# A two-layer graph network on one core: the load of x in 112 + 15 partitions, the copy of src in 128 rows and a rest

## The reference, cut to what matters

```python
h = relu(layernorm(x))
x = x + relu(h @ W_self + segment_mean(h[src], dst) @ W_neigh + b)        # layer 0
h = relu(layernorm(x))
hid = relu(concat(h[src], h[dst]) @ We1 + be1)                            # layer 1, per edge
m = sigmoid(hid @ We2 + be2) * h[src]
msgs = concat(segment_max(m, dst), segment_sum(m, dst))
x = x + relu(concat(msgs, h) @ Wn1 + bn1) @ Wn2 + bn2 + h
```

## Time and profile before

| | us |
|---|---|
| median of 3 runs | 8183.52 |
| lowest and highest of them | 8175.11 and 8204.45 |
| the profiled execution's own time | 8185.29 |
| its span | 8183.6 |

### The profile page before, as it was taken

One profiled execution on the slowest core, in us unless ns is written; L12 is line 12 of the kernel. 1 busy time (PEld: TensorE's weight loads), 2 busy tenths in 40 slices (PEclk: granted clock), 3 DMA queues, 4 the chain that ended last, 5 costly groups with the idle time before them and its releaser, 6 DMA issues.

```text
span 8183.6 us, 111687 instructions
## 1 busy us (share of the span) xinstructions
PE 3724.8 (46%) x24938; PEld 3291.0 (40%) x24939; DVE 4329.6 (53%) x8524; ACT 2902.3 (35%) x4472; POOL 3814.0 (47%) x3768
## 2 busy tenths in 40 slices
PE   0006999999963333333433433333333333343341
PEld 0005888888853333333333333333333333333331
DVE  2746888888854444444544444445444444444441
ACT  4005888888852222222222222222222222222220
POOL 2461000000026666565555555556555555555555
PEclk9999999999975555555555555555555555555555
DMA  3320000000012222222222222222222222222221
GB/s 109 100 48 21 19 18 19 19 19 19 19 40 68 68 65 67 66 67 67 63 66 66 63 64 66 66 63 66 63 64 65 61 62 65 62 65 64 62 65 27
DMA packets 298529, 455.47 MB, mean 56 GB/s; under 512 B 124801, under 2 KB 220264, under 8 KB 298336
## 3 DMA queue, kind: packets, MB, share of 16 engines
q0 software_dynamic: 178784, 375.77, 17.2%
q1 hardware_dynamic: 88308, 50.07, 2.2%
q10 hardware_dynamic: 31402, 29.21, 1.1%
HBM read 385.93 MB, written 40.42 MB: 52 GB/s over the span
## 4 chain that ended last, share of the span: by engine, by line
another core or an unknown queue 25%; PE 24%; issue 17%; DVE 16%; DVEq 9%; ACT 5%; DMA 1%; POOL 1%; ACTq 1%; SPq 0%; POOLq 0%; PEld 0%
PE ps_acc L1378 8%; PE ps_acc L1408 8%; PE ps_pairs L1400 6%; DVE act_w L1108 5%; DVEq L402 4%; DVE chunk_max L1125 3%; ACT counts_f L1267 3%; DVE msg L1119 2%; DVEq L1119 1%; DVE pre L1102 1%; DVEq L1167 1%; DVE z L1114 1%; DVEq L1102 1%; POOL out_dram L533 1%
## 5 line engine op out<-in xcount | busy, mean ns | idle before, releaser
L458 POOL DMA_INDIRECT counts_f<-hA_table,stage x3264 | 3287.2, 1007 | 2346.4 <-issue 971.1
L1378 PE MATMUL ps_acc<-msg,ident 128*128 128x64 f32 (+1 forms) x6508 | 1633.7, 429 | 2536.9 <-DVE msg L1119 2109.9
L1378 PEld LDWEIGHTS ps_acc<-msg,ident 128*128 128x128 f32 x6508 | 1462.1, 326 | 2708.4 <-DVE msg L1119 2025.4
L1267 ACT ACTIVATE counts_f<-ps_pairs 128x784 bf16<-128x784 f32 x1568 | 1270.1, 823 | 311.4 <-PE ps_pairs L1400 244.8
L1119 DVE TENSOR_TENSOR msg<-counts_f,gate 128x256 f32<-128x256 f32 x851 | 359.5, 422 | 1719.8 <-remote 1494.2
L1343 ACT ACT_TABLE_LOAD x834 | 1070.0, 1283 | 259.0 <-DMA own<-own_rows 174.5
L1343 ACT ACTIVATE gate<-z,be_col 128x4 f32<-128x4 f32 x851 | 253.1, 297 | 2232.6 <-DVE z L1114 1584.5
L1408 PE MATMUL ps_acc<-pieces_f,counts_f 128*128 128x192 bf16 x9604 | 1014.6, 246 | 0.7 <-ACT counts_f L1267 0.4
L1400 PE MATMUL ps_pairs<-hot 128*128 128x196 bf16 x6272 | 818.3, 252 | 142.4 <-ACT counts_f L1267 136.2
L521 POOL DMA_INDIRECT hA_table<-node,node_id x98 | 131.8, 1345 | 1610.0 <-ACT node L1278 1575.6
L1408 PEld LDWEIGHTS ps_acc<-pieces_f,counts_f 128*128 128x128 bf16 x9604 | 879.4, 138 | 1.4 <-issue 1.3
(11 more groups left out here) (206 smaller groups left out, 2997.3 us busy)
## 6 DMA issues: line engine op xcount, KB each, us to landing
counts_f<-hA_table,stage POOLq DMA_INDIRECT x3264
counts_f<-counts_f SPq DMA_DIRECT2D x102, 288.0 KB
own_rows<-node ACTq DMA_DIRECT2D x98, 128.0 KB
own<-own_rows ACTq DMA_DIRECT2D x98, 128.0 KB
xh<-records SPq DMA_DIRECT2D x98, 64.0 KB, 1.8
stage<-stream SPq DMA_DIRECT2D x206, 8.0 KB
h_table<-counts_f ACTq DMA_DIRECT2D x14, 224.0 KB
stream<-runs_m SPq DMA_DIRECT2D x14, 224.0 KB
```

The costliest lines, as they stand in the source:

```text
L458: return pool.indirect_dma_start(to, None, table, bass.IndirectOffsetOnAxis(ap=idx, axis=axis))
L1267: act.activation(counts[:, c, nodes, :].rearrange("p (b h) t -> p b (h t)", h=2), ps_pairs[g & 1][:, :].rearrange("p (b w) -> p b w", b=BA ...
L1378: return pe.matmul(ps_sum[:, 0:D], ident[:, :], rows, start=False, stop=False, skip_group_check=True)
```

## The change

The one load of x by 127 partitions becomes two, of 112 and of 15 partitions; the one copy of src becomes one of 128 rows of 3222 numbers and one of the last 84. The two constants that are waited for grow by 16 each. Nothing else differs.

```diff
-        TAB_DMAS = 16 * 2
-        X_DMAS = 16 * (2 if REST else 1)
+        TAB_DMAS = 16 * 3
+        X_DMAS = 16 * (3 if REST else 2)
...
-            sp.dma_start(x_nodes[0:FULL], x[0:FULL * T, :].rearrange("(p t) d -> p t d", p=FULL)).then_inc(s_x, 16)
+
+            by = FULL // 16 * 16
+            sp.dma_start(x_nodes[0:by], x[0:by * T, :].rearrange("(p t) d -> p t d", p=by)).then_inc(s_x, 16)
+            sp.dma_start(x_nodes[by:FULL], x[by * T:FULL * T, :].rearrange("(p t) d -> p t d", p=FULL - by)).then_inc(s_x, 16)
             if REST:
                 sp.dma_start(x_nodes[FULL:FULL + 1, 0:REST], x[FULL * T:N, :].unsqueeze(0)).then_inc(s_x, 16)
             flat_src = src_pad.rearrange("a b -> (a b)")
-            sp.dma_start(flat_src[0:E], src[:]).then_inc(s_tab, 16)
+            even = E // P * P
+            sp.dma_start(flat_src[0:even].rearrange("(a b) -> a b", a=P),
+                         src[0:even].rearrange("(a b) -> a b", a=P)).then_inc(s_tab, 16)
+            sp.dma_start(flat_src[even:E].unsqueeze(0), src[even:E].unsqueeze(0)).then_inc(s_tab, 16)
```

## The result

The changed kernel takes 8082.34 us (median of 4 runs, 8065.82 to 8086.67) against 8193.99 for the kernel before (4 runs, 8175.11 to 8205.71): a ratio of 0.9862, 95% interval 0.9836 to 0.9889. It is faster by 1.4%, between 1.1 and 1.6%. The forecast was 8079. The profiled executions stand at 8086.67 and 8185.29, 98.6 us apart; the medians are 111.7 us apart.

What follows compares the result with a forecast made beforehand. One DMA engine carrying all of x was taken to pace the search for 150 us; the last gather at 163 instead of 268.81 us saves 106, so 8185.3 - 106 = 8079 us, range 8055 to 8120.

Steps and rivals of the forecast that it cites:

- The turn of 1.51 us: Search gathers, kernel before: one piece of x and one gather packet alternate on the loaded engine, 12.1 / 8 = 1.51 us.
- first rival: Load of x: the fifteen rows go to one engine, busy until about 44 us; 8087 us, chance 0.05.
- the upper bound: Load of x, kernel before: 127 pieces at 1.18 us beside gathers, from about 13 us, end at 163 us.
- Fifteen rows on fifteen engines: Second load of x: its 15 partitions give one more piece to each of fifteen engines.
- x by 22.4 us, SP's queue empty by 26: Start: eight pieces of x per engine take 9.4 us from 13; src then takes 3.8 us.
- the worse case of the prediction: Start: x at 255 GB/s takes 12.5 us, so x is in at 25.5 us and SP's queue empty at 29.
- The free pace of 1.40 us: Rest of the search: 89 gathers at 1.40 us each, 124.9 us, from the eleventh at 36.8 us.
- Behind the search: From last gather to end: the remainder of 7914.8 us moves forward whole, keeping the 106 us gain.
- Swallowed: Behind the search: a wait read as slack is not, above all ACT's weights; up to 8185 us, chance 0.05.
- no gain: Load of x: splitting by partitions gains nothing, both parts using the same sixteen engines; 8185 us, chance 0.02.
- slower: Layer 1: two more SP instructions delay its 102 gather groups; 8283 us at 2 us a group, chance 0.02.
- The pace of 2.0 us beside ACT's passes: Search: gathers take 2.0 us with ACT at work, last at 215 us, gain 54, 8131 us; chance 0.04.

Runs made afterwards that it cites:

- the dose of 66 pieces: Changed kernel with x loaded in 64, 61 and 2 partitions instead of 112 and 15: 7980.74 us, against 8021.41 for the kernel before.
- halves: Kernel before, with x as two loads of 49 columns, each of 127 partitions: 6719.33 us against 6731.68.
- quarters: Kernel before, with x as four loads of 24 or 25 columns, each of 127 partitions: 6703.45 us against 6731.68.
- the late load: Changed kernel with x, still split in 112 and 15, loaded only after the search's last gather landed: 7911.93 us against 8021.41 for the kernel before, ratio 0.9871.
- the late whole load: Changed kernel with x loaded after the search as one load of 127 partitions: 7998.38 us against 7914.56 for the changed kernel.

## Why the prediction was right

*The cause.* One engine with 127 pieces of x, taking turns with every gather. Shown from both sides: moving the cut by one partition brings the pairs 12 us apart back, splitting src alone leaves them, the dose of 66 pieces has them without a long hold of SP, and the length of the pieces sets their distance.

*The turn of 1.51 us.* The mechanism was right and this figure of it was not: it came from dividing the 12.1 us of a pair by eight packets. The DMA view of the kernel before from 47.1 to 52.8 us, when the other fifteen engines have nothing left to do, shows the loaded engine by itself:

```profile
DMA packets 10, 0.15 MB, mean 26 GB/s; under 512 B 1, under 2 KB 1, under 8 KB 5
q1 hardware_dynamic: 5, 0.13, 5.1%
q0 software_dynamic: 5, 0.02, 0.9%
```

Five pieces and five packets of gathers, in strict turn: a piece takes 0.94 us and a packet of 5,000 bytes 0.19, a turn of 1.13. One of the five packets is not data but 4 bytes long, and takes next to nothing. With it a gather has five packets on the engine and a pair ten, so ten pieces of x pass with each pair. The packet records from 42.8 to 54.8 us have these ten turns: five of 1.13 us (or 1.12), two of 0.94, and three longer ones of 1.63, 1.63 and 1.24 us while the next pair moves on the other engines, 12.0 us in all. The forecast did not hang on the 1.51, save for the backlog of its first rival; the expectations for halves and quarters did. For the same reason x ended a little beyond the 163 us of the upper bound, at 167.4, or 1.21 us a piece.

*Fifteen rows on fifteen engines.* Right: the packet records have fifteen of these pieces in flight together, in the changed kernel (at 23.9 us) as in the late load. The Trainium skill ("DMA: Bandwidth & Descriptors", section on why a DMA increments its semaphore by 16) states the rule, the largest number up to 16 that divides the slowest dimension, here the rows. All cuts tried agree: 127, 113 and 61 behave like one engine, 112 and 64 like sixteen, 63 like nine, 15 like fifteen. The advice of the Trainium skill (same page, rules for kernel authors) against cutting a transfer by partitions did not hold here, with a ratio of 0.9848 for x alone; it presumes that the whole transfer already uses sixteen engines.

*x by 22.4 us, SP's queue empty by 26.* Here a term was mis-sized. Even the 266 GB/s of the best five us are near the low bound of 255 and far from the single engine's rate times sixteen; x took 15.1 us instead of 9.4 (11.9 to 27.0; alone in the late run 14.8), and the large pieces of src lasted to 32.0. Both ends lie beyond the worse case of the prediction, 25.5 and 29. It cost nothing, and that is in part luck: ACT's second pass covers up to 34 us, which left 2 us to spare; the eleventh gather left at 37.84 for 36.8, and 37.33 without x.

*The free pace of 1.40 us.* It was (167.12 - 37.84) / 89 = 1.45, so the last gather was 4.1 us later than 163: 1.0 us from the later eleventh gather, and 3.1 from the pace (129.3 us for 89 gathers, against 124.9 and the 1.3 added for the weights).

*Behind the search.* 7917.8 us for 7914.8: the remainder moved forward whole, as said, but for 3 us. With the 4.1 of the search that makes the 7 us between 8079 and the profiled 8086.67. The median, 8082.34, lies nearer, by the spread of the runs. ACT's slack was 78.5 us.

*The rivals.* Swallowed, no gain and slower are excluded by the ratio. The pace of 2.0 us beside ACT's passes did not come; why it stays above POOL's own 1.25 is open (last section). Fifteen rows on one engine is excluded by the packet records.

## What to carry to other kernels

Look at the DMA share of a queue, multiplied by sixteen: a steady 0.85 (beside gathers) or 1.02 (alone, the 6.4% of the late whole load) is one engine, and all three loads with a prime number of partitions tried here, 127, 113 and 61, looked like that. The cost in this kernel was not the load's own length, which was hidden, but that every evenly spread gather beside it finished with the slowest engine. The gain can be estimated as the time of that engine's load, less what the others needed anyway: gathers 11 to 33 took 130 us, and 22 gathers at 1.45 take 32, which leaves 98, and the eleventh itself came 4 us earlier. Before splitting further, see whether the first cut already fits under something else: here 8, 11 or no pieces on an engine ahead of the first gathers put the eleventh at 37.8, 42.0 and 37.3 us.

## What the runs showed of the hardware that was not expected

*Stalls with no releaser.* In the changed kernel VectorE and ACT stand still several times in the search, and the profile names nothing that they wait for. At times they do so together (VectorE stands from 84.5 to 87.1 us, ACT for 1.2 us of it), at times not: ACT went on for most of VectorE's longest such wait. That wait, and ACT's last search count:

```profile
108.66 0.17 DVE L707 TENSOR_SCALAR row<-balance  x1 [4.68 <-issue]
```
```profile
120.86 0.18 ACT L1223 ACTIVATION_READ_ACCUMULATOR hot<-pieces_f,q_mid  x1
```

ACT does the same hundred counts as before and needs 6 us more for them, although it waits for no gather. Nine passes in the kernel before, beside DMA engines that the gathers and x kept busy for 29% (23.6 and 5.3), were 10.1 us each without exception. VectorE has such stalls in the free stretch of the kernel before too, 20 us in all from 177 to 270, so the 1.40 us contain them. In the kernel with halves the free stretch ran without them, 42 gathers in 52.97 us, 1.26 us each, which is POOL's own issue cadence, at a DMA share of 0.85. So full DMA engines alone don't bring them about; but that run was on another chip. What the stalls are was not tried.

*Sixteen engines are not sixteen times one.* A piece of 25,088 bytes took 0.92 us on an engine alone before the gathers, and 0.94 in the late whole load, where one engine carried the 127 pieces in 119 us. With x late and split, sixteen engines carried the same 127 pieces in 14.8 us: eight times as fast, not sixteen. A piece then took 1.70 us on the mean; in the best five us it was 1.5 (16 x 25,088 bytes at 266 GB/s), and the last fifteen took 2.2 to 3.3 us. What sets this limit was not tried.

*Three levels of the same kernel.* The kernel before took 8194, 8021 to 8037, and 6732 us in different groups, and the three groups of experiments ran on three chips. The difference to the last level lies in layer 1. The stretch of the earlier trace rows from 2400 us has 3255 gathers in 5750 us; the kernel with halves, of the last group, has this (columns as in the earlier trace rows) for the whole stage:

```profile
2350.00:6600.00 4250.00, 2158.40 (x8075) 1826.90 (x8074) 2553.12 (x5604) 1401.29 (x1979) 3248.36 (x3280) 0.50 0.33 86
```

TensorE's 8075 matmuls and its busy time are the same within 0.2%, at the same granted clock, but the stage is 1500 us shorter. What waits is different: POOL waits 1375 us for TensorE in the kernel before and 14 us here, and VectorE waits 1494 us there for releasers that the profile can't name. Whether the speed of the gathers is the cause, and the chip the cause of that, was not tried. Whatever is measured in this kernel has to be compared within one group.
